# End of the output projection: order of token sums, banks of the first pairs, statistics' copies and casts on ScalarE

## The reference

```
x = x + 0.5 * ffn(layernorm(x))
x = x + attn(layernorm(x))
x = x + 0.5 * ffn(layernorm(x))

attn: Q = x Wq^T (32 heads of 128), K, V = x Wk^T, x Wv^T (one head), rotary,
      windows of 512 with step 256, sigmoid scores over their sum, two windows
      blended linearly, then out Wo^T
ffn:  x W_base^T + b + 2 * sum over the top 2 of 8 experts of
      gate_e * (x A_e^T) B_e^T        (rank 16, softmax router)
```

## Time and profile before

| | |
|---|---|
| median of 3 runs | 2439.57 us |
| the profiled execution | 2436.0 us |
| its span, slowest core (4) | 2434.5 us |
| spans of the cores | 2422.1 to 2434.5 us |
| mean granted TensorE clock | 0.979 to 0.983 of full speed |
| TensorE busy | 2303.2 us, 95% |
| VectorE, ScalarE, GpSimd busy | 1268.4, 1012.3, 627.4 us |
| memory traffic | 469.83 MB, 193 GB/s on the mean |

### The profile page before, as it was taken

The page is one execution under the profiler, slowest core; times in us unless marked ns, Lnnn a source line. Parts: engine busy times, 40 slices in busy tenths (PEclk is TensorE's granted clock), DMA queues, the critical chain, the costliest instruction groups (busy, mean ns, idle before and its releaser), DMA issues.

```text
span 2434.5 us, 37489 instructions; the slowest of 8 cores (2422.1 to 2434.5 us)
## 1 busy us (share of the span) xinstructions
PE 2303.2 (95%) x13024; PEld 1161.9 (48%) x13256; DVE 1268.4 (52%) x2129; ACT 1012.3 (42%) x1324; POOL 627.4 (26%) x602
## 2 busy tenths in 40 slices
PE   5799999999999979999999999989999998999998
PEld 5584444444444425555555555434444444444444
DVE  4342212212122466666666666578888237556655
ACT  5443222222222316666666666633444343233331
POOL 0113444444442321111111111144555421000000
PEclk8899999999999989999999999999999999999999
DMA  9736554455474873333333333457777897677774
GB/s 311 243 136 211 178 177 163 159 181 186 178 242 151 286 258 104 105 105 105 105 105 105 104 105 105 146 208 256 264 255 264 295 304 250 226 253 244 246 256 146
DMA packets 115754, 469.83 MB, mean 193 GB/s; under 512 B 13680, under 2 KB 13936, under 8 KB 78192
## 3 DMA queue, kind: packets, MB, share of 16 engines
q1 hardware_dynamic: 97648, 408.69, 50.6%
q0 software_dynamic: 17920, 58.73, 6.1%
HBM read 408.65 MB, written 58.72 MB: 192 GB/s over the span
## 4 chain that ended last, share of the span: by engine, by line
PE 84%; DMA 5%; DVE 3%; issue 2%; DVEq 2%; ACT 2%; SPq 1%; POOL 0%; ACTq 0%; POOLq 0%
PE PS L344 29%; PE PS L570 26%; PE PS L1216 16%; PE PS L1274 4%; PE PS L1255 3%; DVEq L49 2%; DMA arena<-xp 1%; PE PS L684 1%; DMA arena<-x1h 1%; PE PS L426 1%; PE PS L666 1%; DMA arena<-wo 1%; PE PS L359 1%; SPq L44 1%; PE PS L710 1%
## 5 line engine op out<-in xcount | busy, mean ns | idle before, releaser
L344 PE MATMUL PS<-arena 128*128 128x512 bf16 x3605 | 816.0, 381 | 9.9 <-DVE arena L460 5.7
L570 PE MATMUL PS<-arena 128*128 128x512 bf16 x2854 | 638.0, 381 | 14.2 <-DVE arena L466 11.0
L272 ACT ACTIVATE arena<-arena 128x2048 bf16<-128x2048 f32 (+1 forms) x332 | 509.9, 1574 | 309.7 <-DMA arena<-wb 137.9
L344 PEld LDWEIGHTS PS<-arena 128*128 128x128 bf16 x3678 | 360.9, 98 | 442.0 <-issue 18.1
L1216 PE MATMUL PS<-arena 128*128 128x512 bf16 x1963 | 539.9, 379 | 3.6 <-issue 0.2
L570 PEld LDWEIGHTS PS<-arena 128*128 128x128 bf16 x2912 | 285.8, 98 | 358.0 <-issue 17.2
L457 DVE TENSOR_TENSOR PS<-PS,arena 128x512 f32<-128x512 f32 x160 | 111.8, 699 | 493.2 <-PE PS L426 459.5
L481 ACT ACTIVATE arena<-arena 128x512 f32<-128x512 f32 x145 | 91.0, 628 | 566.6 <-DVE arena L460 420.2
L1216 PEld LDWEIGHTS PS<-arena 128*128 128x128 bf16 x2048 | 190.1, 98 | 146.6 <-issue 1.6
L1101 POOL TENSOR_TENSOR arena<-arena 128x512 bf16<-128x512 f32 x64 | 81.0, 1266 | 577.9 <-DVE arena L1288 540.2
L1258 ACT ACTIVATE arena<-PS 128x512 bf16<-128x512 f32 x384 | 214.7, 604 | 27.3 <-PE PS L1255 27.2
(11 more groups left out here) (126 smaller groups left out, 1661.9 us busy)
## 6 DMA issues: line engine op xcount, KB each, us to landing
arena<-wb SPq DMA_DIRECT2D x128, 1024.0 KB, 7.6
arena<-wq SPq DMA_DIRECT2D x64, 1024.0 KB, 5.1
arena<-wo SPq DMA_DIRECT2D x64, 1024.0 KB, 6.8
arena<-xp SPq DMA_DIRECT2D x24, 1024.0 KB, 13.3
arena<-xr SPq DMA_DIRECT2D x96, 256.0 KB, 3.0
x1h<-arena POOLq DMA_DIRECT2D x96, 256.0 KB, 3.7
arena<-x1h SPq DMA_DIRECT2D x48, 512.0 KB, 11.8
arena<-x1h SPq DMA_DIRECT2D x64, 256.0 KB, 4.1
```

The lines of the kernel that those rows point to most:

```text
L272: a.activation(d, s, ACT.Copy), ws if j == 0 else [])
L344: tok = pr.emit(PE, lambda t, c=c, b=b, w=w, n=n, fin=fin, r=rhs_t: t.matmul(bank(b), w[c // 16][:, c % 16, :], r[:, c, :], start=(n == 0) ...
L570: tok = pr.emit(PE, lambda q, c=c, last=last: q.matmul(bank(b), w[:, c, :], r[:, c, :], start=(c == 0), stop=last), [bank_free.get(b)] + l ...
```

## The change

The order of instructions, the waits on the token sums and one counter; no arithmetic is changed.

- The waits on the token sums become one for each product: `t_tok` was the last sum of all, waited for by the third product of every pair; now it is a table with the sums that the products 6, 7 and 4 (by name: the third, fifth and sixth issued) read.
- The token sums of the output projection: one piece of k = 0, 1 in the last attention slot in place of two; the rest of k = 0, 1 ahead of (2, 0); then all k = 2, the evacuation of (2, 1), and all k = 3 behind it. The bank counter starts at 2 for the first pair.
- ScalarE: the copies of (29, 0) stand ahead of the casts of tile 31; the end of the block 1 statistics and the two reciprocal square root steps ahead of the casts of the second FFN's tile 2; the casts of the bias and adapter weights (bs) behind the first gate. The loads move with them: tile 3 of the second FFN is now loaded behind the last x2h pieces.
- The last two pieces of centring that GpSimd had (n = 27 and 31) are VectorE's.
- Before the second FFN's pairs: token sums of piece 2 and 3 later, three evacuations ahead of (3, 0), the gate's transpose ahead of (2, 1), and the residual loads in that order.

```diff
@@ pair
+        t_tok = t_tok or {}
-        b6, m6 = product(p.sw[1], T[1], [p.t2, t_tok])
+        b6, m6 = product(p.sw[1], T[1], [p.t2, t_tok.get(6)])
-        b7, m7 = product(p.w(0), T[2], [p.t3])
+        b7, m7 = product(p.w(0), T[2], [p.t3, t_tok.get(7)])
-        b4, m4 = product(p.w(1), T[3], [], low(1))
+        b4, m4 = product(p.w(1), T[3], [t_tok.get(4)], low(1))
@@ last attention slot
-    for j in range(2):
-        tsums(xt_wo, [OT[:, 0], OT[:, 1]], j, [q_pe[NU - 1], o_ev[NU - 4]], (0, 1))
+    tsums(xt_wo, [OT[:, 0], OT[:, 1]], 0, [q_pe[NU - 1], o_ev[NU - 4]], (0, 1))
@@ x2_center
-            eng = POOL if n % 4 == 3 else DVE
+            eng = POOL if n % 4 == 3 and n < 24 else DVE
@@ ahead of the output projection's pairs
-    tsums(xt_wo, xo, 2, att_ws)
-    tsums(xt_wo, xo, 3, [o_ev[NU - 1]], (0, 1))
+    for j in (1, 2):
+        tsums(xt_wo, xo, j, att_ws, (0, 1))
+    t_tok = {6: tsums(xt_wo, xo, 3, [o_ev[NU - 1]], (0, 1))}
     WOP[0].s1()
     wo_group(2, 0)
     WOP[0].s23()
-    for j in (0, 1, 3):
-        t_tok = tsums(xt_wo, xo, j, att_ws, (2, 3))
+    for j in range(4):
+        t_tok[7] = tsums(xt_wo, xo, j, att_ws, (2,))
     hend(WT[2], wo_group(2, 1))
+    for j in range(4):
+        t_tok[4] = tsums(xt_wo, xo, j, (), (3,))
+    ps_n[0] = 2
@@ tiles 29 to 31
-    wcast()
-    WF = {0: hload(wb_h[0])}
     g, mm = wo_last(29, 0)
     wo_lev(29, 0, g, mm)
+    wcast()
+    WF = {0: hload(wb_h[0])}
...
     wo_lev(31, 1, g, mm)
-    wcast()
-    for hf in range(2):
-        load_half(bs_h[...], ...)
     x2_center(3)
@@ second FFN
-    forder = [(0, 0), (1, 0), (2, 0), (3, 0), (0, 1), (1, 1), (2, 1), (3, 1)]
+    forder = [(0, 0), (1, 0), (2, 0), (0, 1), (1, 1), (2, 1), (3, 0), (3, 1)]
...
     r0 = rchain2(0)
-    cast_half(w_end)
-    bb2_tok = cast_half()
-    WF[3] = hload(wb_h[3])
+    wcast()
+    for hf in range(2):
+        load_half(bs_h[...], ...)
...
     g2 = gated(f2, 0, gating(f2, 0, at_, rc2))
+    cast_half(w_end)
+    bb2_tok = cast_half()
...
     x2_center(7)
+    WF[3] = hload(wb_h[3])
...
-    for j in range(1, 4):
-        t_tok = tsums(xt_f2, xc3, j)
+    tsums(xt_f2, xc3, 1)
+    hw2[1] = gtrans(f2, 1, g2)
     hend(WF[2], f2_k(2, 1))
...
-    hw2[1] = gtrans(f2, 1, g2)
+    tsums(xt_f2, xc3, 2)
+    for _ in range(3):
+        f2_b()
+    f2_k(3, 0)
+    t_tok = {6: tsums(xt_f2, xc3, 3)}
     FP[0].s1([ar_end, r1])
-    f2_k(3, 0)
-    pend2.insert(0, pend2.pop())
-    for _ in range(4):
-        f2_b()
+    f2_b()
     FP[0].s23()
```

More of the change, by code:

```diff
@@ L1627, in build @@
     wo_lev(31, 1, g, mm)
-    wcast()
-    for hf in range(2):
-        load_half(bs_h[:, hf * 2048:(hf + 1) * 2048], resh(f2["bb"], (NC, 128))[:, hf * 16:hf * 16 + 16])
     x2_center(3)
@@ L1690, in build @@
     r0 = rchain2(0)
-    cast_half(w_end)
-    bb2_tok = cast_half()
-    WF[3] = hload(wb_h[3])
+    wcast()
+    for hf in range(2):
+        load_half(bs_h[:, hf * 2048:(hf + 1) * 2048], resh(f2["bb"], (NC, 128))[:, hf * 16:hf * 16 + 16])
     x2_center(3)
```

## The result

| | before | after |
|---|---|---|
| median, runs | 2440.39 us, 4 | 2416.93 us, 4 |
| ratio, 95% interval | | 0.9898, 0.9883 to 0.9914 |
| profiled execution, slowest span | 2436.0, 2434.5 us | 2416.99, 2415.5 us (core 5) |
| mean granted clock | 0.979 to 0.983 | 0.982 to 0.986 |

The forecast was 2415.5 us. The total came out; one of its six terms had the wrong sign.

A forecast was written before the change was run, and what follows sets the result against it. TensorE was taken as the bound, busy 2303.2 of 2434.5 us, so time could come only from its stops and slow stretches. Six terms summed to 24.1 us, from the median 2439.57 to about 2415.5 us; range 2407 to 2428.

The forecast's parts named there:

- 1 attention's end: Last attention unit's first combine: two of four token sums ahead leave VectorE, the 2.00 us wait goes; 1.6 us gained.
- 2 first pair: Output projection's first pair: both stops go, 14.9 us, less a 3.3 us wait at the sixth product and slow clock; 9.8.
- 3 copies ahead of casts: ScalarE's statistics copies: stop at (30, 0) goes, 7.55 us, but full DMA holds the later copies; net 0.9, bounds -0.5 and 7.55.
- 4 statistics' end: End of block 1 statistics: ScalarE's copy comes at once, the A product's second half doesn't wait; 2.1 us gained.
- 5 chase over (0, 1): Second FFN's chase: x2h loads come earlier, ahead of tile 3's, so VectorE's speed decides; 5.4 us gained, bounds 1 and 7.4.
- 6 group (3, 1): Ahead of the second FFN's pairs: the 2.69 us wait for bank 3 and its slow clock go; 4.3 us gained.
- Rival (a): DMA has slack, loads come as much earlier as TensorE; copies ahead of casts gain 7.5 us; 2409 us, 14%.
- Rival (b): VectorE and GpSimd hinder each other more, first pair gains 5.5, chase stays with loads, gains 1; 2424 to 2427 us, 18%.
- (c): Sixth product takes over the whole wait, full DMA holds later leads; within 4.9 us of before, 2436 us, 4%.
- (d): Slower: pairs start from another bank and one product of each waits; 2455 us at 1.5 us a pair, 4%.

The follow-up runs named there:

- the second look: The kernel after, unchanged, run again on the same chip as two later kernels; ratio to before 0.9899 (0.9855 to 0.9943).
- tile 1 late: Kernel after with the second FFN's tile 1 weight casts and the load behind them moved behind the copies of (31, 1) and the statistics' end; ratio to before 0.9889.

## Why the prediction was right

Term by term, from the stretches:

| term | forecast | measured | from |
|---|---|---|---|
| 1 attention's end | 1.6 | 1.6 | wait 2.00, now 0.41 |
| 2 first pair | 9.8 | 9.4 | A-C; 9.7 to the hundredth matmul |
| 3 copies ahead of casts | 0.9 | -2.8 | C-H |
| 4 statistics' end | 2.1 | 2.8 | H-I |
| 5 chase over (0, 1) | 5.4 | 5.6 | I-J |
| 6 group (3, 1) | 4.3 | 3.6 | J-K and the first pair behind it, -0.4 |
| sum | 24.1 | 20.2 | |

The medians differ by 23.5 us, the profiled executions by 19.0. The 3.3 us between 20.2 and 23.5 are not in the change's stretches: the profiled execution of before was itself 4.4 us under its median, that of after on it. Part of that stands ahead of A, in the part that both kernels share: before reached A at 1569.8 us on the mean, after at 1571.4, though its wait there is 1.6 shorter; that is the 3.2 by which the mean spans of their cores differ less, 17.0 us. So the total of 24.1 met 23.5 with some luck: the terms' stretches sum to 20.2, 3.9 less than forecast, nearly all of it term 3.

Term 2 held in its working. The sixth product waited 4.04 us for 3.3, the last sums ended at 1616.4 for 1615.5, and the slow clock came. Six sums took 16.93 us for the 14.72 that they took before, which hurt little, since the products ran from banks 2 and 3: on core 5 the third and the fifth product waited 0.54 and 0.76 us, against the forecast of none, and on six of the eight cores neither did.

Term 3 is the step that failed, by 3.7 us, and beyond its lower bound of -0.5. Its first half was right: C-F fell by 5.4. The second half said that TensorE would get the copies of (31, 1) some 2.9 us earlier than before, "having stood some 7 us". It stood 6.94 to 10.47, 9.91 on core 5. Counted from C and on the mean of eight cores, the last cast of tile 1 began at 84.8 us in after (84.1 at the second look), at 83.5 before, at 83.6 with tile 31's casts back, and TensorE got the copies at 87.9 (87.2), 86.6 and 86.7: not 2.9 earlier than before but 1.3 later (0.6). I had let the load come earlier by filling the idle DMA time. It was issued earlier, at 66.2 us behind C for 70.1, but its first half was cast at 81.8 for 80.7: it took 15.6 us from issue to cast for 10.6. The idle time at 60 to 66 us behind C shrank, with a DMA share of 0.98 for 0.90, but brought 1.71 MB for 1.66, and up to 82 us behind C both kernels had moved 26.1 MB. A free share of the DMA engines was not free bandwidth here. Why the load then came 1.3 us later, and not at the old time, is open; which other transfers went ahead of it, no run settles.

Rival (a), 7.5 for term 3, falls with the measured -2.8. Rival (b) had a loss in term 3, though -0.5 and not -2.8, and falls with the terms 2 and 5. Rivals (c) and (d) show nowhere: from K to the end all kernels take 357 to 358 us at full clock. (Rival (c) was also mispriced: the terms 4 and 6 alone are 6.4 us, more than its 4.9.)

Term 5's size was right and its cause half told. I named the earlier loads and VectorE's speed; the run with tile 3's load back says that with the 2.1 MB ahead, C-J is 131.5, before's 131.8, though terms 3 and 4 and the move of GpSimd's pieces stay. Terms 3 to 5 are one account: the time from C to J is the bytes that move up to J, at 320 GB/s, plus what the order wastes, 6.2 us before and 3.1 in after.

## What to carry to other kernels

Where the DMA engines are full, add up the bytes that must land before the next point that waits, and move those that aren't needed there behind it: 2.1 MB of a later tile, 1 MB of residuals and 1 MB of a bias row were worth 5.9, 3.9 and 2.2 us here. Reordering casts and copies alone was worth 2 us or less from C to J, but it had to come first: cutting 2.1 MB gave 1.7 us or less in the old order and about 6 in the new. A small operation in an in-order queue behind a cast that waits for a load is worth moving, but ask at once which load the next one in the queue waits for. If a first product waits for a bank and for an operand, mend both: the bank alone gave 3 to 4 of 9.7 us.

## What the runs showed that I had not expected

- Moving a load to a place with some 10% idle DMA, ahead of the full stretch, lost 3.7 us against tile 1 late and 2.8 by the spans against after, though it was ready long before use. The later issues of the tiles behind it speak for the two staging halves as what was scarce there; they were not varied alone.
- The low clock can set in during a wait or behind it. In after it came some 1.0 us after the restart; with the counter alone, inside the wait, on core 1:

```profile
1604.00:1610.00 6.00, 0.41 (x2) 0.70 0.27 83
1610.00:1613.70 3.70, 0.00 (x0) 0.50 0.00 0
1613.70:1617.00 3.30, 3.21 (x9) 0.55 0.21 79
```

- Six token sums took 16.93 us beside GpSimd's adds for four evacuations, where twelve undisturbed took 14.80, 1.23 each: 9.5 us lost in one stretch of VectorE. Before, the same six took 14.72. The last pair of those adds took 2.10 and 2.24 us where the others took 1.26 to 1.29, so both engines lost time.
